# P.V of a head group in two blocks: the first and second tile of keys behind the eighth bank of scores

## The reference

```python
Q = x @ Wq.T + bq
K = x @ Wk.T + bk
V = x @ Wv.T + bv
...
scores = jnp.einsum('bnqd,bnkd->bnqk', Q, K) * scale
...
attn = jax.nn.softmax(scores, axis=-1)
out = jnp.einsum('bnqk,bnkd->bnqd', attn, V)
...
x = _layernorm(x + _L0_attn_ref(x, L0_attn_Wq, L0_attn_bq, L0_attn_Wk, L0_attn_bk, L0_attn_Wv, L0_attn_bv, L0_attn_Wo, L0_attn_bo), axis=-1)
x = _layernorm(x + _L0_ffn_ref(x, L0_ffn_gate_w, L0_ffn_w1, L0_ffn_b1, L0_ffn_w2, L0_ffn_b2), axis=-1)
```

## Time and profile before

| | us |
|---|---|
| median of 3 runs | 556.04 |
| lowest and highest of them | 553.85, 556.76 |
| span of the profiled execution | 521.5 |
| TensorE matmuls busy in it | 445.9 (86%) |
| VectorE busy | 398.1 (76%) |
| ScalarE busy | 332.2 (64%) |
| GpSimd busy | 282.0 (54%) |

### The profile page before, as it was taken

One profiled execution on the slowest core, in us unless ns is written; L12 is line 12 of the kernel. 1 busy time (PEld: TensorE's weight loads), 2 busy tenths in 40 slices (PEclk: granted clock), 3 DMA queues, 4 the chain that ended last, 5 costly groups with the idle time before them and its releaser, 6 DMA issues.

```text
span 521.5 us, 12373 instructions
## 1 busy us (share of the span) xinstructions
PE 445.9 (86%) x3556; PEld 267.2 (51%) x3589; DVE 398.1 (76%) x974; ACT 332.2 (64%) x809; POOL 282.0 (54%) x455
## 2 busy tenths in 40 slices
PE   6788999999999978999999999986869988884880
PEld 2354444445445433544544544532759877774870
DVE  5987779989988966998899899886787756660192
ACT  4285666865875763687587576584578978881045
POOL 6022234235834732573584475587577777777263
PEclk9999999999999997999999999998979999999796
DMA  5656386533443342343344333113144333331564
GB/s 162 197 156 180 105 286 192 161 117 118 139 142 109 107 155 85 111 130 126 108 124 157 105 91 100 38 49 95 53 120 136 104 104 92 90 90 36 163 208 116
DMA packets 74394, 64.56 MB, mean 124 GB/s; under 512 B 9030, under 2 KB 68685, under 8 KB 74336
## 3 DMA queue, kind: packets, MB, share of 16 engines
q1 hardware_dynamic: 68528, 55.08, 36.3%
q0 software_dynamic: 4512, 8.54, 4.9%
q10 hardware_dynamic: 1296, 0.27, 0.3%
HBM read 36.88 MB, written 25.46 MB: 120 GB/s over the span
## 4 chain that ended last, share of the span: by engine, by line
PE 47%; DVE 13%; issue 10%; DMA 9%; ACT 7%; POOL 6%; SPq 4%; another core or an unknown queue 1%; ACTq 1%; DVEq 0%; POOLq 0%
PE psum L1014 12%; PE psum L996 9%; PE psum L973 9%; DVE nmax L1338 7%; DMA o_dram<-probs,xs 4%; PE psum L981 4%; POOL o_dram L762 3%; PE psum L1033 3%; DMA experts<-o_dram 3%; DMA xs<-xs_dram 2%; PE psum L1040 2%; PE psum L1072 2%; ACT probs L808 2%; PE psum L1199 2%; PE psum L1180 2%
## 5 line engine op out<-in xcount | busy, mean ns | idle before, releaser
L808 ACT ACTIVATE probs<-psum 128x512 f32<-128x512 f32 x320 | 181.9, 595 | 107.4 <-PE psum L996 76.8
L1338 DVE TENSOR_REDUCE nmax<-psum 128x2 f32<-128x1024 f32 (+3 forms) x224 | 197.7, 912 | 32.8 <-PE psum L981 31.3
L686 POOL TENSOR_SCALAR_AFFINE_SELECT probs<-probs 128x256 f32<-128x256 f32 (+1 forms) x192 | 88.8, 488 | 140.2 <-ACT probs L808 139.6
L973 PE MATMUL psum<-kst,qst 128*128 128x512 bf16 (+2 forms) x511 | 111.0, 303 | 6.5 <-DVE nmax L1338 5.9
L996 PE MATMUL psum<-qst,kst 128*128 128x128 bf16 (+3 forms) x480 | 102.0, 297 | 6.8 <-ACT probs L808 3.1
L1014 PE MATMUL psum<-probs,vst 128*32 128x512 f32 (+3 forms) x1024 | 91.0, 452 | 1.7 <-POOL probs L686 1.5
L762 POOL DMA_INDIRECT o_dram<-probs,xs x77 | 78.0, 1013 | 26.0 <-issue 16.9
L981 PE MATMUL psum<-bmask,bident 128*128 128x256 bf16 (+1 forms) x320 | 81.0, 253 | 0.1
L996 PEld LDWEIGHTS psum<-qst,kst 128*128 128x128 bf16 x512 | 39.6, 98 | 71.4 <-ACT probs L808 34.0
L973 PEld LDWEIGHTS psum<-kst,qst 128*128 128x128 bf16 x512 | 47.9, 98 | 33.3 <-DVE nmax L1338 10.2
L917 ACT ACTIVATE hT_sb<-psum,w_cur 128x128 f32<-128x128 f32 x154 | 48.1, 364 | 7.9 <-PE psum L1180 7.2
(11 more groups left out here) (199 smaller groups left out, 558.8 us busy)
## 6 DMA issues: line engine op xcount, KB each, us to landing
kst<-dk SPq DMA_DIRECT2D x62, 128.0 KB, 2.8
qst<-dq SPq DMA_DIRECT2D x31, 256.0 KB, 3.1
xs<-xs_dram SPq DMA_DIRECT2D x77, 66.0 KB, 1.9
experts<-o_dram SPq DMA_DIRECT2D x7, 512.0 KB, 4.6
dk<-k SPq DMA_DIRECT2D x7, 384.0 KB, 3.0
dq<-q SPq DMA_DIRECT2D x7, 384.0 KB, 3.0
xT_sb<-in_xT SPq DMA_DIRECT2D x8, 256.0 KB, 2.8
xTv_sb<-in_xT SPq DMA_DIRECT2D x8, 256.0 KB, 2.7
```

The costliest lines, as they stand in the source:

```text
L686: pool.affine_select(out=view, in_=view, compare_op=ALU.is_ge, fill=0.0, base=0, pattern=[[0, view.shape[1]], [1, P]], channel_multiplier= ...
L808: act.activation(probs[:, c % 2, p, kk * T:(kk + 1) * T], ps_t[:, k % 2, :], ACT.Exp, scale=SCALE).then_inc(S["exp_done"], 1)
L973: pe.matmul(bank[:, at:at + w], qst[:, c, e, P * i:P * i + P], kst[:, c, h, e, 0:w], start=(at == 0), stop=False, skip_group_check=True)
L1338: last = dve.tensor_reduce(o, i, AX.X, ALU.max, negate=True)
```

## The change

One table of numbers changes. The first tile of P.V moves from the end of step 6 to step 7, where it is joined to the second in one call of `pv`. Only TensorE's order moves; the lists of the four others are the same.

```diff
         M_AT = 3
-        PV_AT = {6: (0,), 7: (1,), 9: (3, 2)}
+        PV_AT = {7: (0, 1), 9: (3, 2)}
         PV_MASKS = {0: 4, 1: 4, 3: 5, 2: 6}
```

## The result

| | before, us | after, us | ratio, 95% interval |
|---|---|---|---|
| median of the runs (9 each) | 556.04 | 560.14 | 1.0072 [1.0047, 1.0096] |
| lowest and highest | 553.21, 557.19 | 556.16, 561.58 | |
| span of the profiled execution | 521.5 | 558.6 | |
| first exponential of group 0 to first of group 31 | 323.48 | 329.44 | |
| from there to the end | 172.06 | 202.79 | |

What follows compares the result with a forecast made beforehand. TensorE was taken to bound the attention part, busy 39.71 of 41.47 us per batch. The terms sum to +2.5, less 0.1 for VectorE's gain: span 521.5 to about 523.9, plus 34.5 around it, 558.4 us, range 553.4 to 562.0.

Steps and rivals of the forecast that it cites:

- eight c=1, c=2 of batch 0, c=0 of batch 4: Ten attention groups where nothing stands at TensorE's three gates: each saves 0.21 us, together -2.1.
- eleven groups with a `take_off` behind bank 6: Groups c=3 and c=0: TensorE idles 0.54 us for ScalarE's part, less 0.21 saved: +0.33 each, +3.6 together.
- c=2 of batches 1 to 6: Unit 3 waits 0.13 us for VectorE's reduction, less 0.21 saved: -0.08 each, -0.5 for six groups.
- c=3 of batch 6: No `take_off` here; unit 3 waits 0.88 us for VectorE's reduction, less 0.21 saved: +0.7.
- c=0 of batch 7: Unit 3 waits 0.26 us for VectorE's reduction, less 0.21 saved: 0.
- c=2 of batch 7: No units left, ScalarE sets the pace; bank 7 waits for its exponential, bank 8 starts later: +0.8, between 0 and 0.8 open.
- The same: Outcome class: time within about 0.5%, 2.8 us, of the kernel before; chance 0.47, slower 0.41, faster 0.12.
- The saving of the joint block: On TensorE, one P.V block fewer saves 0.13 us in the block and 0.08 for the entry: 0.21 per group.
- the half saving: Rival: the joint block still pays part, half of 0.21 us stays in 30 groups; 561.5 us, chance 0.15.
- The cover of the `take_off`: Before the second `take_off`, tile 0 no longer fills TensorE's wait for ScalarE: 0.54 us idle, bank 6 to bank 8 3.61.
- The waits are absorbed: Rival: TensorE's losses at c=3 and c=0 come back because the next stage waited for another engine; 553.4 us, chance 0.15.
- the gates stand open: Rival: ScalarE's second part is ready once bank 6 is issued, so no `take_off` wait; 552.5 us, chance 0.08.

Runs made afterwards that it cites:

- experiment 9: The kernel before, P.V in three blocks, with only the second `take_off` of q and k moved behind score unit 3; 551.90 us against 552.93, ratio 1.0001.
- experiment 5: The kernel after once more, no edit, beside its variants; 556.65 us against 552.51 for the kernel before, ratio 1.0061.
- experiment 2: The kernel after with the joint block one step earlier, behind bank 6; 525.72 us, ratio 1.0048 to the kernel before.
- experiment 3: The kernel after with the second `take_off` of q and k moved behind score unit 3; 521.05 us, ratio 0.9960 to the kernel before.
- Experiment 4: The kernel after with VectorE's product L1419 moved from step 2 to step 4 of c=2, all batches but the last; 524.22 us, ratio 1.0015.
- experiment 11: The kernel before with only VectorE's product L1419 moved from step 2 to step 4 of c=2, all batches but the last; 552.74 us, ratio 1.0007.
- experiment 6: The kernel after with both the second `take_off` behind unit 3 and L1419 later; 549.88 us against 552.51 for the kernel before, ratio 0.9950.
- experiment 10: The kernel before with the joint block in one group only, c=2 of the last batch; 553.65 us, ratio 1.0009.
- experiment 7: The kernel after with late `take_off`, late L1419 and three P.V blocks in four groups without cover; 546.65 us against 552.51 before, ratio 0.9883.
- experiment 8: The kernel after with P.V in three blocks again in one group only, c=2 of the last batch; 554.67 us, ratio 1.0039 to the kernel before.
- experiment 1: The kernel before once more, no edit, with a profile; 523.25 us against 523.17 for the kernel before on this chip.

## Why the prediction was right or wrong

The terms, with what they measured. "Measured" is the period in the kernel after's first profile less that of experiment 9, whose P.V stands in three blocks. That both have the same chip-related differences is assumed; c=1 of batch 7, +0.48 in the one and +0.40 in the other, supports it.

| term of the prediction | forecast | measured |
|---|---|---|
| eight c=1, c=2 of batch 0, c=0 of batch 4 | -2.1 | -2.8 |
| eleven groups with a `take_off` behind bank 6 | +3.6 | +3.5 |
| c=2 of batches 1 to 6 | -0.5 | +2.2 |
| c=3 of batch 6 | +0.7 | +0.7 |
| c=0 of batch 7 | 0 | 0 |
| c=2 of batch 7 | +0.8 | +0.6 |
| **sum** | **+2.5** | **+4.3** |

The traces' own difference, corrected for the one period that experiment 9's edit changes (c=0 of batch 0, 0.64), is 329.44 - 325.16 = 4.3, and the medians differ by 4.1 twice. That the two agree so well is partly luck: with experiment 5's profile of the same kernel the difference is 6.7, by two stretches at half clock (c=0 of batch 4, c=2 of batch 7).

**The time** was forecast 1.7 us too low and inside the range; the sign and the size of the largest term were right. It came this close partly by luck: one term missed by 2.7, and the misses of the others, the ten groups and c=2 of batch 7, had the opposite sign and took 0.9 of it back. "The same", the likeliest class by a little, was not what came: 1.0072 is beyond the 0.5% border, though the interval starts at 1.0047.

**The saving of the joint block**: forecast 0.21, measured 0.24 in the groups where nothing else moves. The rival of the half saving is dead. The estimate by the Trainium skill that stood beside it ("TensorEngine Tiling (Array Packing)", Key Properties, with the drain of "TensorE: Matmul & The Clock Gate", its step-by-step) was 0.11 a group; an exit and an entry of the 32-column blocks cost twice that here. The ten groups together gave 0.7 more than forecast, most of it in c=0 of batch 4 (-0.84), the group at half clock; the same kernel's second profile had +0.10 there against experiment 9. That is the clock's scatter, not a gain.

**The cover of the `take_off`**: the step was right to the hundredth in batch 4, 3.61 from bank 6 to bank 8. Experiments 2 and 3 show it from both sides: give the cover back, or move what needs it, and +0.33 becomes -0.24, in ten of the eleven places in experiment 2 and in four in experiment 3, where the others keep a part of the loss. "The waits are absorbed" and "the gates stand open" are refuted by the same rows.

**c=2 of batches 1 to 6 is the step that failed**, by 2.7 us. The prediction took the end of the reduction, 223.47, from the trace of before and let only TensorE move against it. It did see that VectorE would get unit 3 up to 1.0 us sooner at c=1, and booked that as a small gain. It did not follow VectorE's lead one queue further: the statistics behind unit 3 feed GpSimd's chain, GpSimd has masks in its list behind that chain, and in four of the six batches these now ran beside VectorE's product, in the other two the issue of a transfer did; the product took 0.30 to 0.83 in place of 0.20, 2.0 us more over the six. Experiment 4 (the product elsewhere: -3.3 us in these groups) and experiment 11 (the same edit without the change: nothing in these groups) settle that the product is where it was lost. How the other 0.7 of the 2.7 us came about is not worked out.

**c=2 of batch 7**: the waits were sized rightly. At full clock, in the kernel after's first profile (timeline, TensorE; the answer to the earlier trace rows), bank 6 to bank 8 is 3.21, against 2.42 before and 3.26 by the forecast:

```profile
350.12 0.39 PE L996 MATMUL psum<-qst,kst 128*128 128x512 bf16 x1 [0.28 <-ACT probs L808]
351.37 0.39 PE L996 MATMUL psum<-qst,kst 128*128 128x384 bf16 x2 [0.86 <-ACT probs L808]
351.69 1.71 PE L1014 MATMUL psum<-probs,vst 128*32 128x512 f32 x16
353.33 0.61 PE L996 MATMUL psum<-qst,kst 128*128 128x384 bf16 x4
```

In the profiles of experiments 2 to 6 and 10 the period was 2.1 to 2.9 longer than before's, because the joint block or the banks around it lay in a stretch at 1.2 GHz. Here is that of experiment 5's profile, which covers the block (windows; the granted clock is third from the end):

```profile
349.61:356.44 6.83, 5.97 (x32) 1.57 (x35) 4.04 (x16) 4.18 (x10) 3.53 (x6) 0.50 0.25 72
```

Of the seven profiles with a joint block in this group, six have such a stretch in it; of the six with three blocks only that of experiment 7 has. So the stretch falls here more often with the change. In the kernel before one comes later instead, behind the first exponential of group 31 (361.45 to 364.86, granted 0.50). Whether the change adds time by it or only moves it stays open: for one edit and its reverse, experiments 8 and 10 give 2.0 and 0.7 us by the medians, 1.2 and 0.5 by the ratios, and neither interval excludes the other.

**What lies around the span** was wrong: 34.5 us forecast, 1.7 to 2.2 measured. It did no harm, since the same constant stood on both sides of the sum.

## What to carry to other kernels

Merging two small blocks of work removes a fixed cost (0.24 us here) and also removes the cover that the first of them gave; move what waits there at the same time, and the change turns from +0.7% to -0.4%, and with the other two repairs to -1.2%. Of these gains 0.64 us, 0.1%, is the one at c=0 of batch 0 that the old order could have had too. When a change lets an engine run ahead, follow that lead through every engine that it feeds until it ends at one that waits: the gain of 0.7 us at one queue became a collision at the next. In stretches where nothing covers a block, keep the old order.

## What the runs showed of the hardware

- VectorE's product of two SBUF operands with 56 columns takes 0.20 us alone and up to 0.83 beside GpSimd's masks; in 41 of 44 such executions it ends 0.07 to 0.08 after a mask does. Beside an indirect transfer's instruction on GpSimd it took 0.20 or 0.43, by when it started.
- The same program takes 523, 553 or 556 us in three settings, at least two of which are different chips; whether it is the chip or something else of the setting no run separates. In the first the part from the first exponential of group 31 to the end takes 172.0 us in the kernel before, and in the others 198 to 203 in all kernels, while in the attention part mainly six periods differ, by 1.55 us together. The granted clock is one part of it (windows of that tail, the kernel after's first profile, then experiment 1):

```profile
355.86:558.60 202.74, 136.28 (x995) 120.41 (x996) 98.47 (x324) 105.19 (x349) 114.76 (x134) 0.87 0.32 90
```

```profile
349.31:521.30 171.99, 126.81 (x995) 111.68 (x996) 100.25 (x326) 105.03 (x348) 117.40 (x136) 0.91 0.37 108
```

TensorE's busy time explains 9.5 of the 30.8 us, so TensorE waits longer too; what for, the traces don't say, and no run of this study tests it.
- P.V's joint block takes 1.64 us at 2.4 GHz and 3.15 at 1.2 GHz. A single such stretch in one profile moves a group's period by up to 1.7 us (c=0 of batch 4, experiments 5 and 8, where the order is the same), more than any term of this change in one group, so periods were read over several kernels.
